# Starting the row gathers of a tile one tile earlier in a two-layer graph network kernel

## The reference, cut to what matters

```python
h = relu(layernorm(x));  z = h @ W                      # layer 1: graph attention, 8 heads
a = exp(leaky_relu(el[src] + er[dst]) - emax[dst])
x = x + segment_sum(z[src] * a, dst) / segment_sum(a, dst) + bias
h = relu(layernorm(x));  s, v = h @ W_up                # layer 2: scalars and vectors
w = silu(silu(edge_feats @ A1 + b1) @ A2 + b2) @ A3     # radial weights of every edge
m = [s[src]*y_s*w0, (v[src].y_v)*w3, s[src]*y_v*w1, v[src]*y_s*w2]
x = x + (segment_sum(m, dst) / 10) @ W_out
```

## Time and profile before

| | |
|---|---|
| median of 3 runs (lowest to highest) | 4855.97 us (4851.73 to 4856.16) |
| the profiled execution | 4860.6 us |
| its span, first to last instruction | 4858.4 us |
| gathers of layer 1, first to last start | 88.5 to 2420.8 us |
| gathers of layer 2, first to last start | 2446.9 to 4834.2 us |
| gathers in a layer | 1568 (196 tiles of 8) |

### The profile page before, as it was taken

How to read it: one execution, slowest core, us unless ns; L and a number is a source line. 1 busy time by engine, 2 the same in 40 slices (tenths; PEclk the granted TensorE clock), 3 DMA queues, 4 the chain that set the end, 5 groups by cost and what they waited for, 6 DMA issues and landing times.

```text
span 4858.4 us, 43517 instructions
## 1 busy us (share of the span) xinstructions
PE 2816.5 (58%) x11218; PEld 2050.7 (42%) x11219; DVE 2517.3 (52%) x6576; ACT 1018.9 (21%) x1447; POOL 3030.4 (62%) x3146
## 2 busy tenths in 40 slices
PE   2444444444444444444467777777777777777776
PEld 2333333333333333333345545455555554445454
DVE  7333333333434334333356666666666666666565
ACT  3222222222222222222221111111111111111111
POOL 2666666666666666666656666666666666666665
PEclk8665666566666566666678888888888888888888
DMA  3111111111111111111111111111111111111111
GB/s 104 50 51 49 52 49 52 52 52 48 52 52 51 52 53 51 52 52 50 50 43 51 47 49 46 49 48 50 49 51 49 49 50 48 47 49 49 47 47 39
DMA packets 139864, 246.43 MB, mean 51 GB/s; under 512 B 54124, under 2 KB 85974, under 8 KB 139734
## 3 DMA queue, kind: packets, MB, share of 16 engines
q0 software_dynamic: 100352, 218.57, 16.3%
q1 hardware_dynamic: 39352, 26.89, 1.9%
q10 hardware_dynamic: 144, 0.80, 0.1%
HBM read 236.02 MB, written 10.03 MB: 51 GB/s over the span
## 4 chain that ended last, share of the span: by engine, by line
POOL 41%; issue 21%; PE 15%; another core or an unknown queue 15%; DVE 4%; DMA 3%; ACT 1%; DVEq 0%; POOLq 0%; ACTq 0%; SPq 0%
POOL rows L436 41%; PE pair L1278 7%; PE pair L1240 2%; PE pair L1234 2%; DMA rows<-up_tab,idx 2%; PE pair L1230 1%; PE pair L1213 1%; PE pair L1254 1%; ACT share L565 1%; DMA rows<-z_tab,idx 0%; DVE share L1063 0%; DVE share L1057 0%; ACT share L567 0%; PE pair L1126 0%
## 5 line engine op out<-in xcount | busy, mean ns | idle before, releaser
L436 POOL DMA_INDIRECT rows<-up_tab,idx x1568 | 1534.1, 978 | 879.4 <-issue 473.1
L436 POOL DMA_INDIRECT rows<-z_tab,idx x1568 | 1494.9, 953 | 924.9 <-issue 557.4
L1213 PE MATMUL pair<-share,acc 128*128 128x136 f32 x3136 | 755.6, 432 | 1127.2 <-issue 653.8
L1213 PEld LDWEIGHTS pair<-share,acc 128*128 128x128 f32 x3136 | 701.1, 326 | 1263.8 <-issue 720.6
L1278 PE MATMUL pair<-share,acc 128*128 128x256 f32 x3136 | 933.5, 450 | 368.1 <-DVE share L1069 220.1
L1278 PEld LDWEIGHTS pair<-share,acc 128*128 128x128 f32 x3136 | 695.4, 228 | 764.6 <-issue 338.6
L941 DVE TENSOR_TENSOR share<-rows,share 128x64 f32<-128x64 f32 x196 | 46.0, 235 | 1159.2 <-DMA rows<-z_tab,idx 1152.8
L1052 DVE TENSOR_TENSOR share<-rows,y_sb 128x384 f32<-128x384 f32 x392 | 222.3, 567 | 631.9 <-DMA rows<-up_tab,idx 601.0
L1240 PE MATMUL pair<-weights_sb,share 128*128 128x256 f32 x1576 | 412.1, 408 | 130.5 <-ACT share L567 74.3
L1240 PEld LDWEIGHTS pair<-weights_sb,share 128*128 128x128 f32 x1576 | 313.0, 203 | 197.5 <-ACT share L567 87.8
L567 ACT ACTIVATE share<-pair,front_sb 128x512 f32<-128x512 f32 x198 | 136.1, 687 | 1046.3 <-issue 387.6
(11 more groups left out here) (166 smaller groups left out, 2416.6 us busy)
## 6 DMA issues: line engine op xcount, KB each, us to landing
rows<-z_tab,idx POOLq DMA_INDIRECT x1568
rows<-up_tab,idx POOLq DMA_INDIRECT x1568
ef_sb<-in_edge_f SPq DMA_DIRECT2D x50, 128.0 KB
z_tab<-rows SPq DMA_DIRECT2D x7, 504.0 KB, 3.2
y_sb<-in_edge_y SPq DMA_DIRECT2D x50, 64.0 KB
x_sb<-in_x SPq DMA_DIRECT2D x7, 448.0 KB, 6.9
up_tab<-acc SPq DMA_DIRECT2D x49, 64.0 KB
out<-x_sb SPq DMA_DIRECT2D x48, 64.0 KB
```

What stands on the lines that cost most here:

```text
L436: pool.indirect_dma_start(out=rows[:, s, t, 0:width], out_offset=None, in_=table, in_offset=bass.IndirectOffsetOnAxis(ap=indices[:, t:t + ...
L1213: mm = t.matmul(bank[2 + h][:, 0:MW], hot[:, s, i, :], msg[:, h, i, :], start=(i == 0), stop=(i == T - 1))
```

## The change

GpSimd waits for the slot of the tile three in front of it, in place of two. To let three tiles pass at the start, `agg[1]` gets the extra count too, and VectorE's wait in layer 2 counts it in.

```diff
@@ -458,7 +458,7 @@
                         hold(pool, idx_set, done * SETS + q + 1)
                         for s in range(U):
-                            hold(pool, s_l1["agg"][(s + AHEAD) % U], n)
+                            hold(pool, s_l1["agg"][(s + 1) % U], n)
                             gather(s, idx[:, e, s, :], tab, width, s_l1["rows"][s])
@@ -614,7 +614,7 @@
             v.memset(ones[:, :], 1.0).then_inc(G["top_ready"], 1)
-            for s in (2, 3):
+            for s in (1, 2, 3):
                 dve.sem_inc(s_l1["agg"][s], 1)
@@ -1076,7 +1076,7 @@
-                        dve.wait_ge(s_l1["agg"][(s - 1) % U], n + 1 if s == 3 else n)
+                        dve.wait_ge(s_l1["agg"][(s - 1) % U], n + 1 if s >= 2 else n)
```

## The result

The changed kernel is slower: 4911.23 us median of 8 runs (4886.81 to 4925.79), beside 4856.34 us for the kernel before in 8 runs (4850.18 to 4887.35). The ratio is 1.0098, with an interval of 1.0071 to 1.0124. I had forecast 4774 us, so the sign is wrong. The profiled execution of after took 4910.61 us, its span is 4908.6.

A forecast was written before the change was run, and what follows sets the result against it. The prediction took GpSimd's gathers to set the pace, with only the time between them removable. Gains of 28 and 67 us less costs of 12 and 1 gave 82 us, hence 4774 us, range 4740 to 4822.

The forecast's parts named there:

- The pause: GpSimd between tiles: stops of about 3.5 us every 16 gathers, 97 a layer, whatever the sums do; not removed.
- The sum: Whole kernel: gains of 28 us in layer 1 and 67 in layer 2, less 12 and 1, make 82 us.
- 1.9-us gaps: GpSimd, after the gather behind every sixth pause: 1.90 us instead of 0.30; up to 16 more in layer 2, 12 us taken.
- The wait: GpSimd at tile borders: true waits for the sum two tiles back, 6 in layer 1, 22 in layer 2; excess over pauses removable.
- mark of 0.83 us: GpSimd's start 0.83 us after the awaited sum's end marks a true wait; elsewhere the start lies 1.3 to 8 us behind.
- Whether they come back: Layer 2 after a double block: no new waits three tiles back save a few; closest has 5 us of room.
- What it costs: VectorE's edits hide in its 601 us of waiting; extra gaps cost 12 us, longer gathers in layer 2 cost 1 us.
- third rival: Layer 2 gathers slowed by the port shared with VectorE: 5044 us, slower once a gather averages over 1.03 us; chance 0.03.
- The first, idle time that comes back elsewhere: GpSimd waits three tiles back or pauses longer: about 4815 us, at worst no change; chance 0.08 within 10 us of old.
- the pause is the semaphore after all: GpSimd at tile borders: pauses go with the waits, both layers lose 367 and 406 us, 4082 us at the most; chance 0.02.
- What would show it: Profile signs: TensorE under 15 us a layer as releaser, about 97 pauses; wrong if layer 2 gathers average over 1.0 us.
- D: Own drain, the prediction's view of GpSimd: it pauses about 3.6 us for its own transfers every 16 gathers, whatever the sums do.

The follow-up runs named there:

- e5: The change in both layers plus the bounded loads, against the kernel before in a held batch (kernel before 4854 to 4866 us): 4989 us, ratio 1.0263.
- f2: The same kernel as e5 run again, the change in both layers plus the bounded loads, against the kernel before in a held batch: ratio 1.0253.
- g2: Distance three in layer 2 only, two in layer 1, plus the bounded loads, against the kernel before in a held batch: ratio 1.0201.
- g1: Distance three in layer 1 only, two in layer 2, plus the bounded loads, against the kernel before in a held batch: ratio 1.0216.
- i2: The same kernel as e5, the change in both layers plus the bounded loads, against the kernel before in a quick batch (kernel before 4302 us): ratio 0.9553.
- e3: Distance three in layer 2 only plus the bounded loads, against the kernel before in a quick batch: ratio 0.9623.
- f1: Distance three in both layers, bounded loads, and GpSimd waits after every odd slot until its own rows land, against the kernel before, held batch: 4840 us, ratio 0.9978.
- g4: As f1, with a loop of eight register loads added to each stop of GpSimd, making stops of 8.8 us on average: 5791 us.
- i1: Control: the kernel before with the bounded loads alone, against the kernel before in a quick batch, beside i2: ratio 0.997.
- bounded loads: Edit in all follow-up kernels: the two limits of a loop over blocks are loaded one by one; alone, 0.997 of the kernel before in quick batches.
- e1: Control: the kernel before with the bounded loads alone, against the kernel before in a quick batch: ratio 0.997.

## Why the prediction was wrong

**The pause** is the step of the mechanism that failed, and with it the price of the gathers (below), the term of the sum that was furthest off. I wrote of tile 74 that "the semaphore had thus been raised 2.2 us before GpSimd even came to the wait", and called the pause a drain "whatever the sums do". I had read the raising off the end of the matmul. Its own record is at 1007.18, 5.0 us behind that end, and GpSimd was waiting for exactly this. The row had said so: its releaser was "remote", not "issue". The view had found a change of an awaited semaphore just before the start, only with no instruction to put it to. That the pause came every 16 gathers was no law of the transfers; 16 was the distance of two tiles, which this change makes three.

**The sum.** Layer 1 came out at 31 us less for the 28 forecast, but not by these terms: its waits fell by 15 us and not 28, and "issue" by 12, because there were 7 of the 1.9-us gaps in place of 14. That the number fits is luck. In layer 2 the forecast had 67 us less of waits, 12 more of gaps and 1 more of gathers, 54 us less in all. Measured were 37 less of waits, 34 more of "issue" and 78 more of gathers. The gathers are the greatest part of the miss.

**The wait.** This was right as a mechanism. In a quick batch, where the sums' increments are on time, GpSimd's long waits are gone (6.6 us to 0.3), and layer 1 became 30 us shorter for the 28 forecast. Layer 2 should have become 67 us shorter. It became 69 longer in the held batch, and 135 shorter where nothing was held. Telling true waits from pauses by the mark of 0.83 us was an error of the same root: 0.82 us is the distance from the recorded increment to GpSimd's start, at tile 74 as well.

**Whether they come back.** "5 us of room" measured from the sum's end. With increments of the sum up to 15.0 us late in layer 2 it was no room. The 601 us of slack that I had given VectorE went too: its waits for rows shrank, and waits for TensorE and for blocks took the place (in layer 1 for `spread`, `er` and line 910, in layer 2 at line 990), of up to 22.6 us. So in layer 2 VectorE often comes to a tile whose rows have long landed, beside gathers in full run.

**What it costs.** The 1.9-us gaps in layer 2 came (16 of them, 12 us taken). The gathers of layer 2 did not cost 1 us more but 78 (1612 for 1534), 1028 ns each, just under the third rival's 1.03. All of it stands in the 65 long ones; the others take 966 ns on average, for 978 before. The other held kernels with distance three in layer 2 and no stops have them too (57 in e5, 58 in f2, 52 in g2), those with distance two, the kernel before and g1, have none. With nothing held there are 12 in i2 and 9 in e3. Of the kernels with stops f1 has 68 and g4 none. In i2 the gathers stand closer together still and take 973 ns, against 969 in i1, so closeness alone is not the cause. In the changed kernel 28 of the 32 that start 0.3 to 0.6 us into VectorE's messages of a tile are long, so it matters where they meet; in the kernel before only four start there. Why they meet there when increments are held isn't shown. The Trainium skill, "SBUF — State Buffer", says in "Who interferes with whom" that the port pair is locked for a whole instruction, against a GpSimd instruction that reads SBUF when VectorE's has two SBUF inputs. The trace agrees in part: 64 of the 65 long gathers end just after VectorE's operation at line 1069, which reads one of its inputs from `pair` and not from SBUF, but line 1053 reads from `pair` too and doesn't end them. No run here moves VectorE's work to test it.

**The rivals.** The first, idle time that comes back elsewhere, happened in part (30 us more of waits at borders are left in layer 2 than forecast), but I priced it at no change at worst. The third, longer gathers beside VectorE, with a chance of 0.03, is what layer 2's time shows, in 65 places and not in all. The second, "the pause is the semaphore after all", had a chance of 0.02 and was right about what the pause is. It was wrong only that the pause goes with a longer distance: a wait further back makes a longer run and a longer hold. Where the increments are on time, its 4082 us is close to the 4110 of i2, which has next to no waits at borders left (45 us).

**What would show it.** Of my own signs, "remote" for about 97 pauses was off (82 and 44 places), and the "wrong" sign of a layer 2 gather over 1.0 us came true.

What is shown: D is refuted. With this change in held batches TensorE's increments are late by up to 26.7 us in layer 1 instead of 13.0, and other engines wait in those times. Longer stops of GpSimd shorten the delays, longer runs lengthen them, and with no delay the kernel with the change gains 4.5%. Layer 2's loss stands in long gathers beside VectorE. What is only argued: that the late increments bring those gathers about. What is open: why a batch is held or quick, what holds an increment and what lets it out in the middle of a run, and the share of the bounded loads in the 1.02 of g1 and g2. One rival wasn't tested. The traces of quick batches have about 61 600 records of semaphore changes and those of held ones 17 400 to 29 800, for kernels that make nearly the same changes; the recording itself may have a part in what is held. No version here beats both kernels in both sorts of batch: the change is best in quick ones (4110 us), and in held ones f1 can't be told from the kernel before.

## What to carry to other kernels

When a wait ends well after its producer has ended, look at when the semaphore was changed, by its record, before calling the rest a property of the waiting engine. Match records by the semaphore that the instruction itself names, in each kernel anew. A wait that looks useless may set the length of a run, and so limit how long other engines' signals are delayed; when it is relaxed, look for the new waits on all engines, and at the longest instructions and not only the median. And run a control in each batch, the one that carries every edit of the test: the same kernel had two times 13% apart, and this change has opposite signs in them.

## What the runs showed of the hardware that I had not expected

- The same kernel took 4302 us in some batches and 4856 us in others, each sort within 2% (single runs 4294 to 4311, and 4811 to 4905). GpSimd's waits at the borders of tiles are 774 us in the held trace of the kernel before and 218 in e1 (quick, with the bounded loads), 556 of the 568 us between their spans. TensorE's increments in layer 1 are 0.02 us late at most in the quick one, and 3.2 to 4.3 us in the median and up to 13.0 in the held one. The granted clock of the two layers is 0.62 and 0.85 in the held trace, 0.64 and 0.88 in e1.
- In held batches many of TensorE's increments reach the others in bursts, typically 3 to 4 us after GpSimd's last gather of a run, but others come out within a run. Stops of 3.2 us on average are too short to let all of them out (90% up to 16.3 us in layer 1), stops of 4.5 suffice there for most (5.0 to 5.3).
- ScalarE's and VectorE's increments in layer 1 were on time beside them, 0.01 to 0.02 us, but for a few records of `msg0` and `msg1` in e5, f2 and g1 (up to 1.9 us).
- An indirect gather that usually takes 0.94 us took up to 3.16 us beside VectorE's operations in unbroken succession, 65 times in layer 2 of the changed kernel.
